# Linear attention with its state products in quarters of the array

## The reference

```python
q = _phi((h @ wq).reshape(b, s, H, DH), proj)     # _phi(x, proj) = elu(x @ proj) + 1
k = _phi((h @ wk).reshape(b, s, H, DH), proj)
v = (h @ wv).reshape(b, s, H, DH)
def step(carry, qkv_t):
    kv, ksum = carry
    q_t, k_t, v_t = qkv_t
    kv = kv + k_t[..., :, None] * v_t[..., None, :]
    ksum = ksum + k_t
    num = jnp.einsum('bhd,bhde->bhe', q_t, kv)
    den = jnp.einsum('bhd,bhd->bh', q_t, ksum) + 1e-06
    return ((kv, ksum), num / den[..., None])
attn = jnp.moveaxis(outs, 0, 1).reshape(b, s, H * DH) @ wo
```

## Time and profile before

| | us |
|---|---|
| median of 3 runs | 3504.65 |
| lowest and highest | 3501.28, 3507.82 |
| the profiled execution's own time | 3525.97 |
| its span in the trace | 3523.8 |
| linear attention's turns in the span | about 1086 to 1830 |

### The profile page before, as it was taken

How to read it: one execution, slowest core, us unless ns; L and a number is a source line. 1 busy time by engine, 2 the same in 40 slices (tenths; PEclk the granted TensorE clock), 3 DMA queues, 4 the chain that set the end, 5 groups by cost and what they waited for, 6 DMA issues and landing times. The chain is left out here.

```text
span 3523.8 us, 62735 instructions
## 1 busy us (share of the span) xinstructions
PE 3297.7 (94%) x22656; PEld 2395.6 (68%) x22656; DVE 2404.2 (68%) x5247; ACT 1563.5 (44%) x3124; POOL 1736.7 (49%) x2205
## 2 busy tenths in 40 slices
PE   8898889888668999999999989999999999999999
PEld 5766667666557888888876656666655566666565
DVE  7999999999754656555654447777633377777333
ACT  6877778876342222222221135555411255555111
POOL 6888899888451000000012247777611277777221
PEclk9999999999889999999999999999999999999999
DMA  4011001111251000010012211112021111121221
GB/s 144 1 63 63 33 31 63 63 57 47 95 171 41 14 12 12 13 36 13 12 51 72 69 60 37 37 38 64 28 73 54 60 34 37 37 73 31 62 65 35
DMA packets 166985, 176.33 MB, mean 50 GB/s; under 512 B 22757, under 2 KB 150265, under 8 KB 166297
## 3 DMA queue, kind: packets, MB, share of 16 engines
q1 hardware_dynamic: 163272, 162.94, 14.3%
q0 software_dynamic: 3408, 9.38, 0.7%
HBM read 94.19 MB, written 78.09 MB: 49 GB/s over the span
## 5 line engine op out<-in xcount | busy, mean ns | idle before, releaser
L3090 ACT ACTIVATE win_probs<-win_sc,win_nbias,tile_rn 128x256 f32<-128x256 f32 x512 | 281.9, 560 | 310.4 <-DVE win_nbias L3174 310.4
L438 POOL TENSOR_TENSOR ssm_acc<-ssm_acc,ssm_weighted 128x512 f32<-128x512 f32 x255 | 339.0, 1339 | 104.5 <-ACT ssm_weighted L587 103.9
L424 POOL TENSOR_SCALAR ssm_ub<-ssm_uT,ssm_bcT 128x512 f32<-128x512 f32 x512 | 359.3, 726 | 25.0 <-PE ssm_pu L1151 21.1
L1151 PEld LDWEIGHTS ssm_pu<-ident,ssm_ub 128*128 128x128 f32 x2048 | 241.2, 143 | 182.7 <-issue 86.4
L1151 PE MATMUL ssm_pu<-ident,ssm_ub 128*128 128x128 f32 x2048 | 312.6, 282 | 49.2 <-DVE ssm_state L821 32.7
L3276 PE MATMUL win_pa<-win_w_wqkv,tile_hT 128*128 128x512 f32 x744 | 358.6, 619 | 0.0
L1167 PE MATMUL ssm_pt<-ident,ssm_state 128*128 128x128 f32 x2040 | 281.0, 280 | 48.4 <-DVE ssm_acc L831 30.5
L1999 POOL TENSOR_TENSOR lin_rstd<-lin_mv,lin_eps 128x1 f32<-128x1 f32 x30 | 5.7, 191 | 627.4 <-DVE lin_mv L173 627.4
L821 DVE TENSOR_TENSOR_SCAN ssm_state<-ssm_da,ssm_carry,ssm_pu 128x512 f32<-128x512 f32 x256 | 312.6, 1263 | 2.4 <-ACT ssm_da L575 2.3
L2692 PE MATMUL glu_up<-block_hT,glu_w_w 128*128 128x512 f32 x704 | 305.7, 592 | 3.4 <-DVEq L88 3.4
L821 DVE TENSOR_TENSOR_SCAN ssm_state<-ssm_da,ssm_pu 128x512 f32<-128x512 f32 x256 | 296.9, 1200 | 6.6 <-PE ssm_pu L1151 4.4
(11 more groups left out here) (422 smaller groups left out, 7294.3 us busy)
## 6 DMA issues: line engine op xcount, KB each, us to landing
sorted_rows<-block_zeros SPq DMA_DIRECT2D x8, 4290.0 KB, 16.5
block_wide<-x SPq DMA_DIRECT2D x18, 512.0 KB, 6.2
tile_raw<-in_tables SPq DMA_DIRECT2D x64, 128.0 KB, 2.2
a<-tile_y SPq DMA_DIRECT2D x64, 128.0 KB, 1.7
block_wide<-a SPq DMA_DIRECT2D x32, 256.0 KB, 3.2
block_x<-a SPq DMA_DIRECT2D x16, 512.0 KB, 5.4
block_x<-sorted_rows SPq DMA_DIRECT2D x39, 130.0 KB
x<-block_more SPq DMA_DIRECT2D x16, 256.0 KB, 2.2
```

The source lines that it names most:

```text
L424: nc.gpsimd.tensor_scalar(ub[:, i % 2, t, :], uT[:, k % 2, t, :], bcT[:, k % 2, t, n:n + 1], 1.0, ALU.mult, ALU.mult).then_inc(ub_ready.se ...
L438: nc.gpsimd.tensor_tensor(acc[:, k % 2, t, :], acc[:, k % 2, t, :], weighted[:, j, :], ALU.add)\
L1151: last = nc.tensor.transpose(pu[c][:, t * P:(t + 1) * P], ub[:, i % 2, t, c * P:(c + 1) * P], ident)
L3090: nc.scalar.activation(probs[:, head, :], sc[j][:, r, :], ACT.Exp, bias=nbias[:, g, j, r:r + 1], scale=rn[:, turn.side, 0, head:head + 1], ...
```

## The change

Pairs 0 to 6 (14 heads) are treated apart from pair 7. For them the state product is done one head at a time, with only that head's 64 partitions of q as weights and its 64x65 state as the moving operand: a weight tile of 64 rows and 64 columns, a quarter of the array. Two heads times two token halves are the four quarters. Even heads add into `pc0`, odd heads into `pc1`. All 28 state products of these pairs come first, then their 28 value products, which are as before but for the place of the output. Pair 7 follows in `pc2`, as before.

DVE takes the banks as 7 even heads, 7 odd heads and 2 heads, and writes `attn` and `den` with a stride. The first two banks' semaphore steps come at the end of the value products of pair 6. The deltas of the 14 heads wait until DVE has read both banks. The state update is 2 operations of 64x7x65 and 2 of 64x65, where it was 4 of 64x3x65 and 2 of 64x2x65.

```diff
-    BANKS = [(0, 3), (3, 6), (6, 8)]
+    LAST = PR - 1
+    BANKS = [slice(0, 2 * LAST, 2), slice(1, 2 * LAST, 2), slice(2 * LAST, H1)]
...
-                for c, (lo, hi) in enumerate(BANKS):
-                    dve.wait_ge(delta_ready.sem, delta_ready.at(i, c + 1))
-                    for j in range(2):
-                        half, cols = slice(j * DH, (j + 1) * DH), slice(j * VW, (j + 1) * VW)
-                        bank = pc[c][half, 0:(hi - lo) * 2 * VW].rearrange("p (r e) -> p r e", e=2 * VW)
-                        last = nc.vector.scalar_tensor_tensor(
-                            state[half, lo:hi, cols], state[half, lo:hi, cols], keep[half, turn.side, :],
-                            bank[:, :, cols], ALU.mult, ALU.add)
-                    last.then_inc(state_ready.sem, 1)
+                for j, half in enumerate(HALVES):
+                    dve.wait_ge(delta_ready.sem, delta_ready.at(i, j + 1))
+                    rows = state[half, 0:LAST, j * VW:(j + 1) * VW]
+                    nc.vector.scalar_tensor_tensor(
+                        rows, rows, keep[half, turn.side, :], pc[j][half, 0:LAST * VW].rearrange("p (r e) -> p r e", e=VW),
+                        ALU.mult, ALU.add).then_inc(state_ready.sem, 1)
...
-                for c, (lo, hi) in enumerate(BANKS):
-                    pe.wait_ge(state_ready.sem, state_ready.at(i - 1, c + 1))
-                    if c == 2 and more:
-                        pe.wait_ge(phi_ready.sem, phi_ready.at(i + 1, 3))
-                    for r in range(lo, hi):
-                        at = (r - lo) * 2 * VW
-                        for half in HALVES:
-                            nc.tensor.matmul(pc[c][half, at:at + 2 * VW], qkT[:, side, 0, r, half], state[:, r, :],
-                                             start=True, stop=False, skip_group_check=True)
-                        for j in range(2):
-                            for half in HALVES:
-                                last = nc.tensor.matmul(pc[c][half, at + j * VW:at + (j + 1) * VW],
-                                                        scores[:, 2 * r + j, half], v[:, side, 2 * r + j, :],
-                                                        start=False, stop=(j == 1), skip_group_check=True)
-                    last.then_inc(num_ready.sem, 1)
+                pe.wait_ge(state_ready.sem, state_ready.at(i - 1, 2))
+                for r in range(LAST):
+                    for j in range(2):
                         for half in HALVES:
+                            nc.tensor.matmul(pc[j][half, r * VW:(r + 1) * VW], qkT[HALVES[j], side, 0, r, half],
+                                             state[HALVES[j], r, j * VW:(j + 1) * VW], start=(r == 0), stop=False,
+                                             skip_group_check=True)
+                for r in range(LAST):
+                    for j in range(2):
+                        for half in HALVES:
+                            ins = nc.tensor.matmul(pc[j][half, r * VW:(r + 1) * VW], scores[:, 2 * r + j, half],
+                                                   v[:, side, 2 * r + j, :], start=False, stop=True,
+                                                   skip_group_check=True)
+                        if r == LAST - 1:
+                            ins.then_inc(num_ready.sem, 1)
+                pe.wait_ge(state_ready.sem, state_ready.at(i - 1, 3))
+                if more:
+                    pe.wait_ge(phi_ready.sem, phi_ready.at(i + 1, 3))
...
                 pe.wait_ge(k_rows_ready.sem, k_rows_ready.at(i))
-                for c, (lo, hi) in enumerate(BANKS):
-                    pe.wait_ge(attn_ready.sem, attn_ready.at(i, c + 1))
...
+                pe.wait_ge(attn_ready.sem, attn_ready.at(i, 2))
+                for r in range(LAST):
+                    for j, half in enumerate(HALVES):
+                        ins = nc.tensor.matmul(pc[j][half, r * VW:(r + 1) * VW], k_rows[:, r, half],
+                                               v[:, side, 2 * r + j, :], start=True, stop=True)
+                        if r == LAST - 1:
+                            ins.then_inc(delta_ready.sem, 1)
```

More of the change, by code:

```diff
@@ L2120, in body @@
                     statistics(Turn(turn.pair + 1, turn.side))
-                for c, (lo, hi) in enumerate(BANKS):
-                    heads = 2 * (hi - lo)
-                    bank = pc[c][:, 0:heads * VW].rearrange("p (h e) -> p h e", e=VW)
+                for c, heads in enumerate(BANKS):
+                    of = den[:, heads]
+                    count = of.shape[1]
+                    bank = pc[c][:, 0:count * VW].rearrange("p (h e) -> p h e", e=VW)
                     dve.wait_ge(num_ready.sem, num_ready.at(i, c + 1))
-                    nc.vector.tensor_scalar(den[:, 2 * lo:2 * hi], bank[:, :, DH], 1e-6, None, ALU.add).then_inc(den_steps.sem, 1)
+                    nc.vector.tensor_scalar(of, bank[:, :, DH], 1e-6, None, ALU.add).then_inc(den_steps.sem, 1)
@@ L2126, in body @@
                     dve.wait_ge(den_steps.sem, den_steps.at(i, 2 * c + 1))
-                    nc.vector.reciprocal(den[:, 2 * lo:2 * hi], den[:, 2 * lo:2 * hi]).then_inc(den_steps.sem, 1)
+                    nc.vector.reciprocal(of, of).then_inc(den_steps.sem, 1)
                     dve.wait_ge(den_steps.sem, den_steps.at(i, 2 * c + 2))
-                    nc.vector.tensor_tensor(
-                        attn[:, 2 * lo:2 * hi, :], bank[:, :, 0:DH],
-                        den[:, 2 * lo:2 * hi].unsqueeze(2).to_broadcast([P, heads, DH]), ALU.mult).then_inc(attn_ready.sem, 1)
+                    nc.vector.tensor_tensor(attn[:, heads, :], bank[:, :, 0:DH],
+                                            of.unsqueeze(2).to_broadcast([P, count, DH]), ALU.mult)\
+                        .then_inc(attn_ready.sem, 1)
@@ L2142, in body @@
+                dve.wait_ge(delta_ready.sem, delta_ready.at(i))
+                for j, half in enumerate(HALVES):
+                    cols = slice(j * VW, (j + 1) * VW)
+                    last = nc.vector.scalar_tensor_tensor(
+                        state[half, LAST, cols], state[half, LAST, cols], keep[half, turn.side, :], pc[2][half, cols],
+                        ALU.mult, ALU.add)
+                last.then_inc(state_ready.sem, 1)
                 if more2:
@@ new lines, in body @@
+                pe.wait_ge(state_ready.sem, state_ready.at(i - 1, 3))
+                if more:
+                    pe.wait_ge(phi_ready.sem, phi_ready.at(i + 1, 3))
+                for half in HALVES:
+                    nc.tensor.matmul(pc[2][half, 0:2 * VW], qkT[:, side, 0, LAST, half], state[:, LAST, :],
+                                     start=True, stop=False, skip_group_check=True)
+                for j in range(2):
+                    for half in HALVES:
+                        ins = nc.tensor.matmul(pc[2][half, j * VW:(j + 1) * VW], scores[:, 2 * LAST + j, half],
+                                               v[:, side, 2 * LAST + j, :], start=False, stop=(j == 1),
+                                               skip_group_check=True)
@@ L2241, in body @@
                 pe.wait_ge(k_rows_ready.sem, k_rows_ready.at(i))
-                for c, (lo, hi) in enumerate(BANKS):
-                    pe.wait_ge(attn_ready.sem, attn_ready.at(i, c + 1))
[L2244 to L2250, removed]
+                pe.wait_ge(attn_ready.sem, attn_ready.at(i, 2))
+                for r in range(LAST):
+                    for j, half in enumerate(HALVES):
+                        ins = nc.tensor.matmul(pc[j][half, r * VW:(r + 1) * VW], k_rows[:, r, half],
+                                               v[:, side, 2 * r + j, :], start=True, stop=True)
+                        if r == LAST - 1:
+                            ins.then_inc(delta_ready.sem, 1)
                 pe.wait_ge(attn_ready.sem, attn_ready.at(i))
+                for j, half in enumerate(HALVES):
+                    ins = nc.tensor.matmul(pc[2][half, j * VW:(j + 1) * VW], k_rows[:, LAST, half],
+                                           v[:, side, 2 * LAST + j, :], start=True, stop=True)
+                ins.then_inc(delta_ready.sem, 1)
                 for g in range(2):
```

## The result

| | before | changed |
|---|---|---|
| median of 6 runs, us | 3506.69 | 3488.28 |
| lowest and highest, us | 3501.28, 3509.98 | 3484.20, 3490.54 |
| span of the profiled execution, us | 3523.8 | 3487.6 |
| a turn of linear attention, us | 23.43 | 22.85 |

The ratio is 0.9946, 95% interval 0.9936 to 0.9956: by it 18.9 us less (15.4 to 22.4); the two medians lie 18.4 apart. The forecast was 20 us less, 3484; the measured 3488.28 lies in its range of 3477 to 3499.

The account below looks back on a forecast made before the run. TensorE's own pace was taken to bound the kernel: -0.79 for quarters and +0.15 for the change of tile gave -0.64 us a turn, x 32, + 0.4 at the end: -20 us, so 3484 us, range 3477 to 3499.

Parts of the forecast that it names:

- What bounds the kernel: Linear attention: TensorE's own pace sets the turn of 23.43 us; whatever its stream gets shorter by, the turn does.
- The state products: Pairs 0 to 6: 1.59 us a turn removed, 0.80 added as 56 quarter records, so -0.79 us a turn.
- The unknown: State products: whether four quarter tiles run at once, which no trace row showed; between -0.79 and +1.60 us a turn.
- The removed part: Old state products of seven pairs, 0.2275 us each, half of a pair's 0.455: 1.59 us a turn.
- The rival of imperfect overlap: State products: quarters run more than two but less than four at a time, 1.06 us a turn, 3492; chance 0.10.
- that of two at a time: State products: rows and columns can't be shared at once, so no gain, +5 us, 3509; chance 0.08.
- The estimate made from a page of the Trainium skill: State products: the page's 3.07x for four row tiles would give 3.19 / 3.07 = 1.04 us for the quarters.
- The change of tile: Between quarters and value products: one more change of form a turn, 0.10 us pause plus exposed load, 0.15 us.
- The prediction's count of fourteen: Changes of tile: the order pair by pair would pay fourteen times, all quarters first once a turn.
- Deltas: Deltas' wait for both DVE banks: second bank done at 4.7, deltas at 5.06, 0.35 us of slack, cost nothing.
- The last turn: Last turn, without the cover of L2184: deltas wait for two whole banks, about 0.4 us more, once.
- Sum: Whole kernel: -0.64 us a turn, x 32 = -20.5, + 0.4 at the end: -20 us.

Follow-up runs that it names:

- e1: Changed kernel, but each of the 28 state products takes all 128 rows (form 128*64), no quarters: 3509.76 us, ratio 1.001 to the kernel before.
- e4: Changed kernel, but one state product takes all 128 tokens of a head (form 64*128), rows shared, columns not: 3514.52 us, ratio 1.002 to the kernel before.
- e3: Changed kernel, but the quarter products of all even heads come before those of all odd heads: 3508.53 us, ratio 1.0006 to the kernel before.
- e2: Changed kernel, but each pair's quarters are followed by its own value products: 3548.49 us, ratio 1.0117 to the kernel before.
- e6: Changed kernel, but value products of the 7 even heads come before those of the 7 odd heads; another chip, one run: 3505.36 us.
- a_again: The changed kernel unaltered, run again on another chip: ratio 0.9951 to the kernel before, median 3503.70 us.
- e7: e6 with pair 7's state products in quarters too and its last bank taken one head at a time: ratio 0.9943 to the kernel before, 3501.05 us.

## Why the prediction was right

**What bounds the kernel.** Right. A turn shrank by exactly what TensorE's own stretch shrank by, and e1 to e4, which differ in the state products alone or in their order, move the turn by what the stretch from the first state product to L2190 changes: 3.21 us in the changed kernel, 3.87, 5.06, 3.85 and 3.94 in these, and turns of 22.85, 23.51, 24.71, 23.49 and 23.59.

**The state products.** The unknown went the way that was taken: four at a time, 14 steps of 0.058. The term was -0.79 us; it measures -0.74. The removed part was taken as half of a pair, 0.2275. In the changed kernel seven pairs' value products take 1.68 us with 0.055 of an open load, 0.232 a pair, so the state products had only 0.455 - 0.232 = 0.223, 1.56 in seven pairs, and the quarters take 14 x 0.0583 = 0.82, not 0.80. The rival of imperfect overlap (1.06 for the quarters) and that of two at a time are out for this order of the program; e3 shows that two at a time is nearly what another order gives. The estimate made from a page of the Trainium skill, TensorE: Matmul & The Clock Gate, section Measured speedup vs the span model, 1.04 us, is too high here: 0.82 was measured. (The page's row is for four row tiles with 512 columns, not for quarters with 65.)

**The change of tile.** 0.15 was predicted, 0.155 measured in e2. The Trainium skill's rule (TensorEngine Tiling (Array Packing), section Key Properties) was put beside it, that a change of mode drains TensorE; e2 agrees, with 1.86 us for 12 changes. The prediction's count of fourteen for the order pair by pair was off: e2 has that order, and 13 changes a turn, 12 more than the changed kernel.

-1.56 + 0.82 + 0.155 = -0.585 us a turn, where -0.64 was predicted and -0.58 measured.

**Deltas.** Right that they cost nothing in the middle turns: DVE's first bank began at 2.75 as worked out, and L2131 took 0.62 for 448 elements (0.63 predicted). The second bank came at 4.78, not 4.7, and the 0.12 us from DVE's end to TensorE's load was left out, so the slack was 0.22 and not 0.35.

**The last turn.** Here the sum was off. The stretch from its first state product to the MLP's first matmul went from 1831.49 - 1819.01 = 12.48 to 1796.08 - 1782.76 = 13.32 us, 0.84 more. Beside the earlier trace rows, the kernel before has:

```profile
1819.01 0.44 PE L2231 MATMUL lin_pc<-lin_state,lin_space 128*64 128x130 f32 x4 [0.45 <-issue]
...
1831.49 4.10 PE L2692 MATMUL mlp_up<-block_hT,mlp_w_w 128*128 128x512 f32 x9 [1.76 <-DVEq L88]
```

The state and value products themselves are about 0.55 us shorter than before (3.66 to 3.11), so 1.4 us is lost where 0.4 was allowed. The step that failed is "now they wait for two whole banks, about 0.4 us more". Before, 12 of the 16 deltas ran while DVE worked on its second and last bank, and 4 stood behind the wait, from 4.79 us into the turn (1823.80 - 1819.01). Now all 16 stand behind it, from 4.93 (1787.69 - 1782.76). That is 0.14 later with 12 deltas more in the open, 12 steps of 0.058 = 0.70 us: together the 0.84. e6 shows the same wait from the other side: with the first bank ready earlier it is 0.7 us shorter.

**Sum.** 30 turns x 0.58 + 0.57 for the turn before the last - 0.84 = 17.1 us. The trace shows 16.7; the twelfth turn of the changed kernel, at 1331 to 1354 us, is 0.30 longer than its like, with TensorE idle 0.14 before the transpose L2168. It is no accident of one execution: in a_again and in e1 to e6 the twelfth turn is 0.30 longer as well, with the same transpose late, while the kernel before and e7 have no such turn. What causes it stays open. The runs' 18.9 agree within their interval. Forecast and trace differ by 3.4 us: 1.9 from the turns (0.64 taken, 0.58 measured), 1.1 from the last turn, 0.3 from the long one. All three go the same way, so the forecast did not come out by errors that cancel, and the range, made for runs that spread by 3 us, covers them.

## What to carry to other kernels

Small matmuls can use all four quarters of the array at once, but here they did so, a short seam aside, only when four neighbours in the program used four different quarters. In all these kernels even and odd heads also wrote to different banks; whether that is needed, no run here tests. Judge the gain by the steps between starts, since a record's duration (0.22 us) does not change. Put all products of one form together, since each change of form cost as much here as nearly three steps, more than a pair's quarters save. When a bank is made to hold more, look at the turn in which nothing else covers the engine that empties it.

## What the hardware showed that was not expected

- A tile's pace is the slower of stream and weight load, even with two tiles side by side: 65 columns behind a 128-column load went every 0.112 us, behind a 64-column load every 0.058 (e4, e1). That the form 64*128 has the slower pace by itself is the reading that e4 leaves open. I had weighed rows against columns only by the share of the array.
- Quarters with the other rows run ahead of the program's order only a little: e3 had four at a time in three steps at the seam, some 0.2 us, and two at a time in the other 22.
